# TensorE's waits for the next stage at the last passes of the stage in front, and new orders on all engines

## The reference

```python
x = _layernorm(x + _L0_gnn_ref(x, adj, W, b))            # adj @ (x W + b) / row sums
x = _layernorm(x + _L1_gnn_ref(x, adj, nodemask, Wqk, Wv))  # softmax over nodes of q.(adj k), times v
x = _layernorm(x + _L2_gnn_ref(x, adj, adj, Wq, ..., bo, 128))  # 8 heads, scores * (adj + adj), softmax
x = _layernorm(x + _L3_gnn_ref(x, adj, W1, b1, gamma, beta, W2, b2))
# L3: h = relu(hconv(x, W1)); h = layer_norm(h); y = hconv(h, W2); y + x
# hconv: H = (adj != 0); out = D^-1 H B^-1 H^T (x W^T) + b
```

## Time and profile before

| | us |
|---|---|
| median of 3 runs | 1837.02 (1836.42 to 1837.74) |
| the profiled execution | 1836.38 |
| its span, first to last instruction | 1834.7 |
| TensorE busy | 1802.5 (98% of the span) |
| VectorE, ScalarE, GpSimd busy | 1446.6, 1445.7, 1445.5 (79% each) |
| TensorE in the chain that ended last | 95% |
| mean granted clock of TensorE | 0.998 |

### The profile page before, as it was taken

How to read it: one execution, slowest core, us unless ns; L and a number is a source line. 1 busy time by engine, 2 the same in 40 slices (tenths; PEclk the granted TensorE clock), 3 DMA queues, 4 the chain that set the end, 5 groups by cost and what they waited for, 6 DMA issues and landing times.

```text
span 1834.7 us, 52850 instructions
## 1 busy us (share of the span) xinstructions
PE 1802.5 (98%) x15358; PEld 1582.8 (86%) x15358; DVE 1446.6 (79%) x3910; ACT 1445.7 (79%) x4463; POOL 1445.5 (79%) x2857
## 2 busy tenths in 40 slices
...
DMA packets 93590, 62.94 MB, mean 34 GB/s; under 512 B 8430, under 2 KB 92924, under 8 KB 93564
## 3 DMA queue, kind: packets, MB, share of 16 engines
...
...
## 4 chain that ended last, share of the span: by engine, by line
PE 95%; DVE 2%; issue 1%; ACT 1%; POOL 1%; DMA 0%; DVEq 0%; SPq 0%; POOLq 0%
PE ps L476 56%; PE ps L579 7%; PE ps L547 6%; PE ps L539 5%; PE ps L555 4%; PE ps L461 4%; PE ps L492 3%; PE ps L568 3%; PE ps L529 2%; PE ps L486 2%; PE ps L513 2%; DVE z L1061 1%; PE ps L466 1%; ACT z L732 0%; DMA x_in<-in_x_dram 0%
## 5 line engine op out<-in xcount | busy, mean ns | idle before, releaser
L732 ACT ACTIVATE z<-z,z_max 128x128 f32<-128x128 f32 x1024 | 399.2, 401 | 0.1
L833 POOL TENSOR_TENSOR ln_rs<-ln_ve,minus_half 128x1 f32<-128x1 f32 x640 | 352.9, 551 | 50.1
L853 POOL TENSOR_TENSOR z<-z,z_rcp 128x1024 f32<-128x1024 f32 x128 | 243.2, 1900 | 39.4 <-DVE z_rcp L1079 39.4
L836 POOL TENSOR_SCALAR ln_nm<-ln_mv,ln_rs 128x1 f32<-128x1 f32 x640 | 171.0, 267 | 109.6 <-POOL ln_rs L833 109.6
L671 ACT ACTIVATE h<-h,ln_nm,ln_rs 128x512 f32<-128x512 f32 x128 | 104.5, 816 | 155.3 <-POOL ln_nm L836 152.5
L831 POOL TENSOR_TENSOR ln_ve<-ln_mv,eps_col 128x1 f32<-128x1 f32 x640 | 123.1, 192 | 115.9 <-DVE ln_mv L985 115.8
L476 PE MATMUL ps<-w1T,txT 128*128 128x512 f32 x768 | 210.1, 409 | 1.1 <-DVE txT L995 0.9
L476 PE MATMUL ps<-w2T,mnT 128*128 128x256 f32 x1536 | 206.0, 283 | 0.0
L732 ACT ACTIVATION_READ_ACCUMULATOR z<-z,z_max 128x1 f32 x1024 | 203.5, 199 | 0.0
L476 PEld LDWEIGHTS ps<-w2T,mnT 128*128 128x128 f32 x1536 | 192.5, 188 | 9.6 <-issue 0.5
L1061 DVE SCALAR_TENSOR_TENSOR z<-ps,a_hold 128x512 f32<-128x512 f32 x256 | 174.1, 681 | 33.8 <-PE ps L539 25.5
...
## 6 DMA issues: line engine op xcount, KB each, us to landing
x_in<-in_x_dram SPq DMA_DIRECT2D x128, 128.0 KB, 2.1
a_hold<-in_adj_dram SPq DMA_DIRECT2D x128, 128.0 KB, 2.2
out_dram<-y_out SPq DMA_DIRECT2D x128, 128.0 KB, 1.9
a_in<-in_adj_dram SPq DMA_DIRECT2D x128, 64.0 KB, 1.8
...
```

What stands on the lines that cost most here:

```text
L732: m = act.activation(z[:, g % 2, h, :], z[:, g % 2, h, :], ACT.Exp, bias=z_max[:, g % 2, h:h + 1], accum_out=z_sum[:, g % 2, h:h + 1])
L833: pool.tensor_tensor(rs[n][:, g:g + 1], ve[n][:, g:g + 1], minus_half[:, :], ALU.pow).then_inc(root_made[n], 1)
L836: pool.tensor_scalar(nm[n][:, g:g + 1], mv[n][:, g, 0:1], rs[n][:, g:g + 1], -1.0, ALU.mult, ALU.mult).then_inc(shift_made[n], 1)
L853: pool.tensor_tensor(zg, zg, z_rcp[:, g % 2, :].unsqueeze(2).to_broadcast([P, HEADS, P]), ALU.mult)\
```

## The change

1. `early` yields the waits of the next stage that are not for its latest operand: its PSUM bank, its DMA for `at` and `ax`, and operands that are usually long ready (`amT`, the column of `hb`, `v2` for `cx`, `mp` for `tx` and `mn`). `room` takes one of them ahead of each of the last passes of the stage in front: as many passes as the next stage has banks, one more for `at`, `ax` and `cx`, and never ahead of the first pass, except in one-pass stages whose own wait was left out. What finds no place stands at the start of the stage as before.
2. The waits for all weights between first and second walk go; the stages that read `wo`, `w1` and `w2` wait for them in the first walks. `w2` is transposed into `c3` and `x3` instead of `z`; GpSimd waits for `scaled` ahead of its second walk.
3. New orders on all engines. The scores, `z`, maxima and exponentials of graph 0, the scores of graph 1, `v2.0`, `v2.1`, `mp.0` to `mp.2` and `probs.0` are made a round earlier than their readers; the two score stages of a graph always stand next to each other; `cx.2` and `cx.3` no longer do; on GpSimd `c3.0` now stands ahead of `wm.0`.

```diff
 ORDER_TEXT = {
     "pe": """
-        at.0+:5 at.1+:3 v2.1:4 sc1.0:0 sc0.0:6 v2.2:2 at.2+:0 ax.0+:3 sc1.1:1 mp.2:5 at.3+:0 ax.1+:3 h0.0+:4
-        sc0.1:0 sc1.2:5 ax.2+:4 v2.3:7 h0.1+:0 h0.2+:2 ax.3+:4 pt.0:0 sc0.2:2 mp.3:6 cx.0:5 h0.3+:1 x1t.0+:0
-        wo.0:7 pt.1:1 sc0.3:3 sc1.3:5 amx.0+:7 x1t.1+:0 cx.1:2 xg.0+:3 v1.0+:5 tx.0:7 amx.1+:4 x1t.2+:1
-        wo.1:6 amx.2+:0 h1.0:3 x1t.3+:7 xg.1+:1 xg.2+:6 amx.3+:3 xg.3+:2 pt.2:0 pt.3:3 wt.0+:7 tx.1:6 cx.2:1
-        cx.3:4 v1.1+:2 wo.2:1 pb.0+:3 wo.3:4 h1.1:7 v1.2+:1 mn.0:3 tx.2:0 v1.3+:4 tx.3:6 h1.2:0 y.0:5 mn.1:3
-        h1.3:7 x2t.0+:6 y.1:0 mn.2:3 x2t.1+:2 mp.0+:7 v2.0+:6 x2t.2+:5 x2t.3+:1 y.2:4 k0.0+:1 mn.3:4 mp.1+:3
-        q1.0+:2 k1.0+:6 y.3:0 q0.0+:6
+        at.0+:2 at.1+:5 v2.2:6 at.2+:4 at.3+:3 mp.3:1 ax.0+:7 ax.1+:2 pt.0:5 sc1.2:3 sc0.2:0 h0.0+:7 ax.2+:4
+        cx.0:2 ax.3+:6 h0.1+:3 wo.0:7 h0.2+:2 pt.1:0 h0.3+:3 sc1.3:4 sc0.3:6 cx.1:2 x1t.0+:0 v2.3:1 amx.0+:7
+        tx.0:5 wo.1:3 amx.1+:4 x1t.1+:7 pt.2:1 xg.0+:3 h1.0:0 cx.2:5 xg.1+:6 amx.2+:3 x1t.2+:1 wo.2:4
+        amx.3+:3 x1t.3+:0 xg.2+:5 tx.1:1 pt.3:3 xg.3+:7 h1.1:1 wt.0+:3 cx.3:2 v1.0+:7 v1.1+:6 pb.0+:1 wo.3:4
+        tx.2:3 v1.2+:1 v1.3+:7 mn.0:2 h1.2:6 mn.1:0 y.0:5 tx.3:2 x2t.0+:6 x2t.1+:0 y.1:4 x2t.2+:1 x2t.3+:3
+        h1.3:2 q0.0+:6 k0.0+:5 q1.0+:0 k1.0+:7 mn.2:5 mn.3:1 sc1.0+:2 sc0.0+:6 y.2:4 y.3:5 mp.0+:1 mp.1+:2
+        mp.2+:0 v2.0+:7 sc1.1+:3 sc0.1+:5 v2.1+:0
     """,
...
     "act": """
...
+        at.0+ at.1+ at.2+ at.3+ v2.2 mp.3 ax.0+ exp0.1 ax.1+ pt.0 exp1.1 cx.0 ax.2+ exp1.2 ax.3+ exp0.2 pt.1
...
     "pool": """
-        mask.0+ xb.0+ xb.1+ x2c.2 xb.2+ xb.3+ am.0+ probs.0 ln0_root.0+ ln0_root.1+ probs.1 dmax.0 hT.0+
-        ln2_root.0 ln0_root.2+ dinv.0 x2c.3 ln0_root.3+ probs.2 ln2_root.1 probs.3 wm.0+ c3.0 ln3_root.0
-        ln2_root.2 ln2_root.3 hb.0+ x3b.0 ln3_root.1 ln1_root.0+ ln1_root.1+ x3b.1 ln3_root.2 ln1_root.2+
-        ln1_root.3+ x3b.2 x2c.0+ ln3_root.3 x2c.1+ ln4_root.0 ln4_root.1 ln4_root.2 x3b.3 ln4_root.3
+        mask.0+ xb.0+ xb.1+ dmax.0 x2c.2 am.0+ xb.2+ probs.1 xb.3+ ln0_root.0+ ln2_root.0 ln0_root.1+
+        probs.2 x2c.3 ln0_root.2+ dinv.0 ln0_root.3+ ln2_root.1 probs.3 c3.0 wm.0+ ln2_root.2 x3b.0
+        ln3_root.0 ln3_root.1 ln1_root.0+ ln2_root.3 ln1_root.1+ ln1_root.2+ ln1_root.3+ ln3_root.2 x3b.1
+        ln4_root.0 ln3_root.3 hT.0+ ln4_root.1 x2c.0+ hb.0+ x2c.1+ x3b.2 x3b.3 ln4_root.2 ln4_root.3
+        probs.0+
     """,
     "sp": """
-        lh.0+ la.0++ la.1++ store.0 la.2++ la.3++ lx.0++ lh.1+ lx.1++ store.1 lh.2+ lx.2++ lx.3++ store.2
-        lh.3+ store.3
+        lh.1+ lx.0++ la.0++ la.1++ la.2++ la.3++ lx.1++ store.0 lh.2+ store.1 store.2 lx.2++ lh.3+ lh.0++
+        lx.3++ store.3
     """,
...
+PASSES = {"at": 1, "ax": 2, "x1t": 2, "amx": 1, "wt": 1, "pb": 1, "x2t": 2, "mp": 1, "sc0": 4, "sc1": 4, "pt": 8, "cx": 8,
+          "tx": 2, "mn": 4, "y": 12, "turn": 1, "gram": 1, "c2": 1, "bw": 1}
+PASSES.update({s: 6 for s in ("h0", "xg", "v1", "v2", "wo", "h1", "q0", "q1", "k0", "k1")})
...
+            def early(stage, g, a, owners):
+                if stage == "at":
+                    pe.wait_ge(a_loaded[g], (group["now"] + a) * 16 + 16)
+                    yield
...
+                elif stage == "cx" and need(read["v2"], a, g):
+                    yield
+                elif stage in ("tx", "mn") and need(read["mp"], a, g):
+                    yield
+                for other, og, away in owners:
+                    later = ((s, 0 if s in per_group else og, away) for s in FOLLOWS.get(other, ()))
+                    if not any(s in begun for s in later) and need(read[other], away, None if other in per_group else og):
+                        yield
+
+            def room(left, free=False):
+
+                if left < group["passes"] and left <= group["slots"] or free:
+                    next(group["next"], None)
...
                 for k, (c, i, j) in enumerate(passes):
+                    room(len(passes) - k)
                     m = pe.matmul(o, left(i, c), right(j, c), start=(k == 0), stop=(k == len(passes) - 1))
...
+                turns = bank_turns(schedule, previous)
+                waits = iter(())
+                for k, (stage, g, ahead, b) in enumerate(schedule):
+                    for _ in waits if k else early(stage, g, ahead, turns[0]):
+                        pass
...
+                    if k + 1 < len(schedule):
+                        other, og, away, _ = schedule[k + 1]
+                        waits = early(other, og, away, turns[k + 1])
+                        group["slots"] = BANKS[other] + (other in ("at", "ax", "cx"))
...
             walk(FIRST["pe"], -1, ())
-            pe.wait_ge(read["turn"], NT)
-            pe.wait_ge(split_made, len(SPLITS))
             walk(ORDER["pe"], 0, FIRST["pe"])
...
             pool.wait_ge(read["bw"], 1)
+            pool.wait_ge(scaled, C2)
             walk(ORDER["pool"], 0)
```

More of the change, by code:

```diff
@@ new lines @@
+        ln0_norm.0+ cx.1 x1t.0+ ln2_norm.0 v2.3 ln0_norm.1+ amx.0+ tx.0 exp0.3 x1t.1+ pt.2 exp1.3
+        ln0_norm.2+ cx.2 amx.1+ ln0_norm.3+ amx.2+ x1t.2+ ln2_norm.1 relu.0 x1t.3+ amx.3+ tx.1 pt.3 wexp.0+
+        cx.3 relu.1 ln2_norm.2 ln3_norm.0 tx.2 ln3_norm.1 mn.0 ln1_norm.0+ ln2_norm.3 mn.1 relu.2
+        ln1_norm.1+ tx.3 x2t.0+ ln1_norm.2+ ln1_norm.3+ x2t.1+ x2t.2+ x2t.3+ ln3_norm.2 relu.3 hbc.0+
+        ln4_norm.0 k0.0+ q1.0+ q0.0+ ln3_norm.3 k1.0+ mn.2 mn.3 ln4_norm.1 exp1.0+ mp.0+ mp.1+ mp.2+ exp0.0+
@@ L60 @@
+        v2.0+ ln4_norm.2 v2.1+ ln4_norm.3
     """,
     "dve": """
[L62 to L66, removed]
@@ L112 @@
+        turnlo.14+ x2t_lo.1+ x2t_lo.2+ x2t_lo.3+ turnlo.15+ turnlo.16+ c2lo.0+ lo_wo.0+ turnlo.17+ ecnt.0+
+        turnlo.18+ turnlo.19+ scale.0+ scale.1+ z1.0+ zmax1.0+ z0.0+ scale.2+ zmax0.0+ scale.3+ z0.1+ z1.1+
+        zrcp.0+ bwlo.0+ lo_w2.0+
     """,
     "pool": """
-        mask.0+ xb.0+ xb.1+ xb.2+ am.0+ xb.3+ hT.0+ ln0_root.0+ ln0_root.1+ ln0_root.2+ ln0_root.3+ hb.0+
-        rep.0+ half.0+ wm.0+ rep.1+ ln1_root.0+ ln1_root.1+ ln1_root.2+ ln1_root.3+ x2c.0+ x2c.1+
+        xb.0+ mask.0+ xb.1+ xb.2+ xb.3+ am.0+ ln0_root.0+ ln0_root.1+ ln0_root.2+ ln0_root.3+ rep.0+ rep.1+
@@ L116 @@
+        wm.0+ hT.0+ ln1_root.0+ ln1_root.1+ ln1_root.2+ ln1_root.3+ x2c.0+ half.0+ hb.0+ x2c.1+ probs.0+
     """,
     "sp": """
-        la.0+ in_mask.0+ la.1+ lx.0+ la.2+ in_b0.0+ la.3+ lx.1+ lx.2+ lx.3+ lh.0+ in_vec.0+ in_v.0+ lh.1+
-        lh.2+ in_q.0+ in_k.0+ in_bias.0+ in_o.0+ lh.3+ in_w2.0+ in_w1.0+
+        lx.0+ in_mask.0+ la.0+ la.1+ in_b0.0+ la.2+ la.3+ lx.1+ lx.2+ lx.3+ in_v.0+ lh.0+ lh.1+ in_vec.0+
+        in_q.0+ in_w2.0+ lh.2+ lh.3+ in_bias.0+ in_w1.0+ in_k.0+ in_o.0+
     """,
@@ L128 @@
+        h1.3:7 mn.1:5 y.0:4 mn.2:7 y.1:1 mn.3:5 y.2:0 y.3:2
     """,
     "act": """
[L130 to L133 removed]
+        mp.3 exp0.1 pt.0 exp1.1 cx.0 exp1.2 exp0.2 pt.1 ln2_norm.0 cx.1 exp0.3 tx.0 exp1.3 v2.2 pt.2
```

141 lines of the change are left out of this document (75 added, 66 removed).

## The result

Before takes 1836.7 us (median of 4, 1835.6 to 1837.7), the changed kernel 1823.9 us (median of 4, 1823.0 to 1824.3): ratio 0.9929, 95% interval 0.9912 to 0.9947, 12.9 us less. The forecast was 1793 us, 44 us less.

What follows compares the result with a forecast made beforehand. TensorE, 95% of the chain, was taken as the bound, with 2.3 us lost per 56.2 us round. From 1836.38, -41 us over 31 rounds and -3 at the ends gave 1792, forecast as 1793; range 1768 to 1832.

Steps and rivals of the forecast that it cites:

- Part 1: On TensorE, score stages in pairs instead of some alone save 0.55 us a round, between 0.30 and 0.70.
- Part 2: At TensorE stage boundaries, moving the second wait into earlier passes saves 0.46 us a round, between -0.64 and +0.2.
- The bound on the other side: Worse end for early asking on TensorE: +0.2 us a round, if one bank a round is late by a pass.
- Part 3: New orders on all engines remove some real waits: -0.3 us a round, between -1.4 and +1.0; the least certain term.
- the loop: Path probs.0 to wm.0 on GpSimd, TensorE to y.3's end, back to probs.0: 53.8 us a round without waits.
- its last term: From y.3 through VectorE's statistics and aggregate and ln4_root.3 to the next probs.0: 2.8 us with hand-overs.
- the first term: GpSimd's work from probs.0 to wm.0, counted without waits: 26.1 us a round.
- the prediction's own signs of being wrong: wt.0 or pt.0 waiting over 1 us a round, a pass over 0.2 us bank-late, or a round over 55.6 us.
- Edits at nothing: Moved w2 transposes, SyncE loads and GpSimd's x3b.2, x3b.3 and hb.0 were taken to cost nothing.
- Rival 3: c3.0 ahead of wm.0 makes GpSimd's waits land on wt.0; slower from 2.5 us of waits, example 1856 us; chance 0.11.
- Part 4: Last walk -6.5 us, first walk about 2.9 us of added work plus 0.6 of waits; net -3, between -6 and +3.

Runs made afterwards that it cites:

- scores_apart: Changed kernel with h0.3 moved between sc1.3 and sc0.3 on TensorE, splitting one score pair into two lone stages: 1835.5 us.
- old_orders_new_waits: Orders of the kernel before on all engines, with the changed kernel's early asking (not in the last walk): 1902.3 us, ratio 1.0362.
- first_loads_old: Changed kernel with SyncE's first loads in the order of the kernel before: 1823.0 us.
- late_three: Changed kernel with the waits inside ax.1, h0.0 and mp.1 put back to the start of the stage that needs the bank: 1823.5 us.

## Why the prediction was wrong

**Part 1, score pairs: right.** Forecast -0.55 us a round. By the starts of a mid round the score stages went from 3.47 us (without a wait of 0.32) to 3.00, and the passes of all other stages, with the ways in and out, from 50.44 to 50.24: 0.67 us less, and a split pair costs 0.75 where 0.70 was forecast (scores_apart). It was inside its bounds.

**Part 2, the second wait: right mechanism, mis-sized term.** The price at one place is exact, 0.147 to 0.054 us at y.1, wo.0 and pt.0. The failed step is the count: I took 3 x 0.09 and the whole losses of four more places, as if each 0.09 us reached the end of the round. Measured is -0.18 us a round in the old orders, with the late banks left out, and -0.07 (by the rounds; -0.15 by the medians) in the new ones, not -0.46. The bound on the other side was too near: +0.2 for one late bank a round, and old_orders_new_waits shows +2.1.

**Part 3, who is late in the new orders: the loop was right, its last term was not.** Forecast 26.1 + 24.9 + 2.8 = 53.8 us; the trace shows 26.6 + 24.9 + 4.2 = 55.7. The failed step is "2.8 us with hand-overs, as I judge it" for y.3 to probs.0. It counted y.3's own addition, statistics, aggregate and one root, and that isn't the path. VectorE takes y.3 behind z0.0, zmax0.0 and the statistics of y.2, and ln4_root.2 stands in front of ln4_root.3: that makes 3.5 us. y.2, at the head of this row, waited for x3b.2: 0.65 us more. Another 0.5 us are missing in the first term, which had no wait in it: GpSimd waits 0.58 us for zrcp.1 at probs.1. What holds zrcp.1 up no run took apart. So the loop was 0.8 us longer than the forecast round of 54.9 us, 26 us in the 31 rounds (1727.8 against 1702), and no more of what parts 1 and 2 gave could arrive. Waits were to fall by 0.76 us a round with part 2; they rose by 0.15. Two of the prediction's own signs of being wrong are there: passes over 0.2 us late for a bank (0.33 in ax.1, 0.34 in h0.0), and a round over 55.6 us.

**Edits at nothing: wrong for x3b.2.** "y.2 and mp.0 stand behind the four projections and the first scores" compares the step with TensorE's order. The reader, though, is VectorE's y.2, and the step stood behind hT.0 and hb.0 on its own queue. VectorE stood idle for 0.58 us in front of y.2, which follows x3b.2 at once. Moving x3b.2 alone gives 18 us.

**Rival 3: half right.** wt.0 is late behind c3.0 and wm.0, by 0.47 us, as a part of the closed loop, but the waits in front of it are 0.5 us and not the 2.5 from which the kernel would be slower; and swapping the two steps costs 102 us. GpSimd's waits for aggregates and z_rcp did not fall, as the prediction said that they would; in the earlier trace rows they are 4.9 us a round, in after 5.8:

```profile
L902 POOL TENSOR_TENSOR z<-z,z_rcp 128x1024 f32<-128x1024 f32 x128 | 242.9, 1897 | 26.6 <-DVE z_rcp L1129 26.6
...
L880 POOL TENSOR_TENSOR ln_ve<-ln_mv,eps_col 128x1 f32<-128x1 f32 x640 | 121.8, 190 | 160.0 <-DVE ln_mv L1035 157.7
```

**Part 4, ends: one near, one not.** The last walk gave 5.9 us of 6.5, in part by luck: the clock was not in the sum. With the same last walk scores_apart took 46.3 us at a granted clock of 0.88 where after took 44.2 at 0.97; by these two an estimate for before's 0.92 is that some 1 us of the 5.9 is the clock. The first walk cost 8.4 instead of 3.5; TensorE's busy time in it rose by 4.0 us and its idle time by 4.4. I had 0.6 us of idle time. By first_loads_old and late_three about 2.2 us are the order of the first loads and 1.1 the clock, both of which I had at nothing. A wait of 2.2 us in front of the x2T transposes (ln1_norm) is new and was not in the sum either. How the rest divides was not tried.

31 us were missing to the forecast: 26 in the steady rounds and 5 in the first walk. Five steps of GpSimd moved (hT.0, x3b.2, x2c.2, x2c.3, xb.3) give 34 (1823.9 to 1789.9), hT.0 none of them beside x3b.2; the early waits decide 2 to 5 us with the loop closed and 8 with it open.
